# A macaron block on one core: expert blocks taken in packs of up to four instead of one at a time

## What is computed

```python
x = x + 0.5 * ffn(layernorm(x)); x = x + attn(layernorm(x)); x = x + 0.5 * ffn(layernorm(x))
def ffn(x):                      # both times the same weights; 8 experts, H = 512
    probs = softmax(xf @ router_w.T); topv, topi = top_k(probs, 2)
    topv = topv / (topv.sum(-1, keepdims=True) + 1e-9)
    h = gelu(einsum('td,edh->teh', xf, w1), exact)     # only the two chosen experts count
    return sum over the two chosen e of topv_e * (h_e @ w2[e])
```

## Time and profile before

| | us |
|---|---|
| median of 3 runs | 418.84 |
| the runs | 416.03, 418.84, 419.93 |
| the profiled execution | 416.92 |
| its span, first to last instruction | 415.2 |
| first expert phase, about | 25 to 185 |
| attention, both groups, about | 185 to 264 |
| second expert phase, about | 264 to 402 |

### The profile page before, as it was taken

One profiled execution on the slowest core, in us unless ns is written; L12 is line 12 of the kernel. 1 busy time (PEld: TensorE's weight loads), 2 busy tenths in 40 slices (PEclk: granted clock), 3 DMA queues, 4 the chain that ended last, 5 costly groups with the idle time before them and its releaser, 6 DMA issues.

```text
span 415.2 us, 6711 instructions
## 1 busy us (share of the span) xinstructions
PE 278.6 (67%) x1985; PEld 253.5 (61%) x1986; DVE 152.0 (37%) x675; ACT 143.9 (35%) x280; POOL 159.5 (38%) x187
## 2 busy tenths in 40 slices
PE   3226359981399359997376781599718998878650
PEld 2216359971299259985165551499618998878640
DVE  5691015710111013574169651557002221312234
ACT  4212125521154035653133241275114564434220
POOL 4447710067414720007702477001760006566650
PEclk9999559996589658999575787789856999889785
DMA  7913231122195210111100011112211222222115
GB/s 252 321 34 95 52 33 34 34 59 57 44 211 183 58 44 27 38 41 46 52 6 0 2 44 51 47 33 58 83 51 55 76 66 70 59 70 77 57 38 171
DMA packets 34254, 29.33 MB, mean 71 GB/s; under 512 B 4824, under 2 KB 29152, under 8 KB 34224
## 3 DMA queue, kind: packets, MB, share of 16 engines
q1 hardware_dynamic: 29312, 18.65, 15.0%
q0 software_dynamic: 4768, 9.78, 9.8%
q10 hardware_dynamic: 144, 0.52, 0.3%
HBM read 15.68 MB, written 13.26 MB: 70 GB/s over the span
## 4 chain that ended last, share of the span: by engine, by line
PE 51%; another core or an unknown queue 18%; issue 13%; DVE 10%; DMA 3%; ACT 2%; ACTq 1%; POOL 1%; SPq 0%; DVEq 0%; POOLq 0%
PE bank L1073 20%; PE bank L1085 18%; PE bank L1064 3%; PE bank L1143 2%; DVE xs L871 2%; PE bank L1030 2%; PE bank L1123 2%; PE bank L1014 2%; PE bank L1107 1%; PE bank L1133 1%; ACT w_block L567 1%; DVE xa L732 1%; DMA router_rows<-in_L_ffn_router_w 1%; DMA y_rows<-final_rows 1%
## 5 line engine op out<-in xcount | busy, mean ns | idle before, releaser
L1073 PE MATMUL bank<-xT,w_block 128*128 128x128 f32 x736 | 113.8, 300 | 37.8 <-issue 27.0
L1073 PEld LDWEIGHTS bank<-xT,w_block 128*128 128x128 f32 x736 | 102.8, 214 | 41.4 <-issue 36.5
L1085 PE MATMUL bank<-w_sb,act 128*128 x736 | 109.2, 296 | 19.5 <-issue 11.2
L1085 PEld LDWEIGHTS bank<-w_sb,act 128*128 128x128 f32 x736 | 100.0, 211 | 23.9 <-issue 23.9
L573 ACT ACTIVATE act<-bank 128x512 f32<-128x512 f32 x92 | 54.9, 597 | 157.8 <-PE bank L1073 72.1
L857 DVE COPY yb<-bank 128x128 f32<-128x128 f32 x92 | 26.6, 290 | 183.9 <-PE bank L1085 91.6
L500 POOL DMA_INDIRECT y_rows<-slots_out,slot_of x48 | 45.9, 957 | 64.9 <-DMA slots_out<-yb 50.9
L476 POOL DMA_INDIRECT xb_first<-xn_rows,row_in x46 | 43.6, 949 | 57.7 <-issue 42.9
L567 ACT COPY w_block<-w_sb 128x512 f32 x92 | 56.4, 613 | 20.7 <-issue 20.4
L511 POOL DMA_INDIRECT final_rows<-yb,row_of x23 | 22.4, 974 | 52.0 <-DVE row_of L847 38.2
L844 DVE COPY xT<-bank 128x128 f32<-128x128 f32 x92 | 26.1, 283 | 20.4 <-remote 13.4
(11 more groups left out here) (124 smaller groups left out, 243.5 us busy)
## 6 DMA issues: line engine op xcount, KB each, us to landing
slots_out<-yb SPq DMA_DIRECT2D x69, 64.0 KB
w_sb<-in_L_ffn_w SPq DMA_DIRECT2D x8, 512.0 KB, 7.4
xb_numbered<-numbered_slots SPq DMA_DIRECT2D x23, 64.5 KB
slots_in<-w_sb SPq DMA_DIRECT2D x4, 368.0 KB
xb_numbered<-slots_in SPq DMA_DIRECT2D x23, 64.0 KB
numbered_slots<-numbered SPq DMA_DIRECT2D x3, 387.0 KB
xs<-in_L_attn_x SPq DMA_DIRECT2D x4, 256.0 KB, 3.4
out<-xs SPq DMA_DIRECT2D x8, 128.0 KB
```

The lines of the kernel that those rows point to most:

```text
L1073: mm = nc.tensor.matmul(h_ps[k][:, q * P:(q + 1) * P], w1_block[c2 % UNROLL][:, q * P:(q + 1) * P], xT[c2 % UNROLL][:], start=True, stop=True)
L1085: mm = nc.tensor.matmul(y_ps[k][:, 0:D], act[c3 % UNROLL][:, q * P:(q + 1) * P], w2_sb[:, bass.ds(at + q * D, D)], start=(q == 0), stop=(q ...
```

## The change

The 46 blocks of a phase are cut into 14 packs of 1, 2, 4, 4, 4, 4, 4 and 4, 4, 4, 4, 4, 2, 1 blocks; seven packs are a group. A pack has one PSUM bank for its turned rows (there is one such bank, where there were two of one block each) and one for its results (there are two), and each is copied by one VectorE instruction. First products have four banks. `w1_block` and `act` exist eight times, `xT_pack` twice, `xb_pack` and `yb_pack` three times. TensorE makes the first products of pack n with the second products of pack n-1 between them, and turns pack n+1 behind the second first product of pack n. SyncE's loads and stores take a pack each, 256 KB for four blocks. The waits of `gather_in` are once a pack: for the pack four before to have landed, and in group 1 for the turn of the last pack whose buffers it overwrites. In the tail, four gathers come first and then, behind the final stores of each pack, three. All steps are written out; there are no loops. Positions of work beside the steps shift a little, two PSUM banks of the second normalisation and the turned attention weights move, and the products of blocks 2 and 3 of a phase wait for that normalisation's copies. The core of the diff, cut, in the order constants, banks, SyncE, GpSimd (two places), ScalarE, VectorE, TensorE; `turn_at` is 1, and 0 in a pack of one block:

```diff
-LAG = 4
-UNROLL = 4
+PACK = 4
+PACK_SIZES = [1, 2] + [PACK] * 10 + [2, 1]
+H_BANKS = 4
+WIDE_BUFS = 8
+PACK_BUFS = 3
+FETCH_SEMS = 4
...
+        RETURNED_FIRST, RETURNED_BESIDE = 4, 3
...
-        xT_ps, h_ps, y_ps = bank[0:2], bank[2:4], bank[4:6]
+        xT_ps, y_ps = bank[0], (bank[1], bank[4])
+        h_ps = (bank[2], bank[3], bank[5], bank[6])
...
+            def load(n):
+                k, size = n % PACK_BUFS, len(blocks_of(n))
+                if n >= LAST_PACKS + PACK_BUFS:
+                    sp.wait_ge(row_known, n - LAST_PACKS - PACK_BUFS + 1)
+                elif n >= PACKS + PACK_BUFS:
+                    sp.wait_ge(xT_ready, n - PACK_BUFS + 1)
...
+            for n in range(PACKS, LAST_PACKS + 1):
+                if n + 2 < LAST_PACKS:
+                    load(n + 2)
+                if n + 1 == LAST_PACKS:
+                    sp.wait_ge(scattered[1], 16 * TOP * GT)
+                    load(n + 1)
+                    load(n + 2)
+                if n == LAST_PACKS:
+                    load(n + 2)
+                if n > PACKS:
+                    store(n - 1)
+            for n in range(LAST_PACKS + 3, 2 * PACKS):
+                load(n)
...
-                for b in range(MAX_BLOCKS):
-                    c = g * MAX_BLOCKS + b
-                    if c >= UNROLL:
-                        pool.wait_ge(x_fetched[c % UNROLL], 16 * (c // UNROLL))
-                    if g:
-                        pool.wait_ge(xT_ready, b + 1)
+                if g:
+                    pool.wait_ge(xT_ready, pack_of(blocks_of(n)[-1] - MAX_BLOCKS) + 1)
+                if n >= FETCH_SEMS:
+                    pool.wait_ge(x_fetched[n % FETCH_SEMS], 16 * transfers_until(n - FETCH_SEMS, 0, FETCH_SEMS))
+                for c in blocks_of(n):
...
-            for b in range(MAX_BLOCKS):
-                store_final(b)
-                if b % FINAL_PACE:
-                    next(returning, None)
+            some_of(returning, RETURNED_FIRST)
+            for n in range(LAST_PACKS, 2 * PACKS):
+                store_final(n)
+                some_of(returning, RETURNED_BESIDE)
...
+                for c in range(first, end):
+                    gelu(c)
+                    if c + H_BANKS < end:
+                        copy_w1(c + H_BANKS)
+                    beside(c - first + 2)
...
+                for n, turn_at in first_product_at(m):
+                    for j, c in enumerate(blocks_of(n)):
+                        beside(c - first + 2)
+                        if j == turn_at and n + 1 < (m + 1) * PACKS:
+                            copy_xT(n + 1)
+                    if n > m * PACKS:
+                        copy_y(n - 1)
...
+                for n, turn_at in first_product_at(m):
+                    behind = len(blocks_of(n - 1)) if n > m * PACKS else 0
+                    for j in range(max(len(blocks_of(n)), behind)):
+                        if j < len(blocks_of(n)):
+                            first_product(n, j)
+                        if j == turn_at and n < last_pack:
+                            turn(n + 1)
+                        if j < behind:
+                            second_product(n - 1, j)
+                        if j < len(blocks_of(n)):
+                            beside(PACK_STARTS[n] + j - first + 2)
```

More of the change, by code:

```diff
@@ L39 @@
 MAX_BLOCKS = (GT * P * TOP + (P - 1) * E) // P
[L40 to L47 removed]
+OFFSETS = 4
+BLOCKS = GROUPS * MAX_BLOCKS
+PACK = 4
+PACK_SIZES = [1, 2] + [PACK] * 10 + [2, 1]
+assert sum(PACK_SIZES[:7]) == MAX_BLOCKS and sum(PACK_SIZES) == BLOCKS
+PACKS = len(PACK_SIZES)
+GROUP_PACKS = PACKS // GROUPS
+PACK_STARTS = [m * BLOCKS + sum(PACK_SIZES[:n]) for m in range(2) for n in range(PACKS)]
+LAST_PACKS = 2 * PACKS - GROUP_PACKS
+H_BANKS = 4
+WIDE_BUFS = 8
+PACK_BUFS = 3
+FETCH_SEMS = 4
 FILL_PARTS = 4
@@ new lines, in transfers_until, with packs_until, first_product_at, offset_reader @@
+        def transfers_until(n, first, sems):
+            return sum(len(blocks_of(p)) for p in range(first, n + 1) if p % sems == n % sems)
+        def packs_until(n, first):
+            return len([p for p in range(first, n + 1) if p % PACK_BUFS == n % PACK_BUFS])
+        def first_product_at(m):
+            for n in range(m * PACKS, (m + 1) * PACKS):
+                yield n, min(1, len(blocks_of(n)) - 1)
+        def offset_reader(eng, regs, m):
+            known = {}
+            def at(c):
+                b = c - m * BLOCKS
+                if b % MAX_BLOCKS % OFFSETS == 0:
+                    if b == MAX_BLOCKS:
+                        eng.wait_ge(routed, GROUPS * (m + 1))
+                    n = min(OFFSETS, MAX_BLOCKS - b % MAX_BLOCKS)
+                    eng.load(regs[:n], expert_at[0:1, b:b + n])
+                    for j in range(n):
+                        known[c + j] = eng.snap(regs[j], min_val=0, max_val=(E - 1) * H)
+                return known[c]
+            return at
@@ L396, in _ @@
-            first_expert_phase()
-            last_expert_phase()
+            for n in range(PACKS):
+                store(n)
+                if FIRST_FILL <= n < FIRST_FILL + FILL_PARTS:
+                    fill_part(2 * (n - FIRST_FILL))
+                    fill_part(2 * (n - FIRST_FILL) + 1)
+            sp.wait_ge(scattered[0], 16 * TOP * GT)
+            load(PACKS)
+            load(PACKS + 1)
+            for n in range(PACKS, LAST_PACKS + 1):
[9 more added lines that the diff above has]
+                    store(n - 1)
@@ L494, in gather @@
                 g = p % GROUPS
-                for k in range(UNROLL):
-                    done = len([G for G in range((p + 1) * MAX_BLOCKS) if G % UNROLL == k])
-                    pool.wait_ge(y_stored[k], 16 * done)
+                end = (p + 1) * GROUP_PACKS
+                for n in range(end - PACK_BUFS, end):
+                    pool.wait_ge(y_stored[n % PACK_BUFS], 16 * packs_until(n, 0))
                 for t in range(GT):
```

380 lines of the change are left out of this document (168 added, 212 removed).

## The result

The changed kernel took 430.43 us (median of 4 runs, 429.22 to 432.64) against 418.60 for the kernel before beside it (416.03 to 419.93): ratio 1.0296, 95% interval 1.0227 to 1.0365. It is slower by 12 us; the forecast was 416.8, no change, in a range of 404 to 426. Two further measurements of the changed kernel on other chips gave ratios of 1.0298 (c0) and 1.0359 (e0).

What follows compares the result with a forecast made beforehand. It took TensorE to be bound at 1.90 us a block, plus losses beside GpSimd's unbroken indirect transfers. Terms 0 - 2.0 + 0 + 2.5 - 2.5 = -2.0 on 416.92 gave 414.9, or 416.8 as median; range 404 to 426.

Steps and rivals of the forecast that it cites:

- Undisturbed blocks at 1.90: Expert phases away from GpSimd's transfers: a block takes 1.90 us, TensorE is full, and the change leaves this untouched.
- Copies and turns in fours: VectorE copies and TensorE turns per four blocks: hidden behind TensorE, worth 0, range -1 to +2 us.
- Four banks: First products: more banks and buffers give 0 in long runs of transfers, and 0.9 us in each short one.
- short trains: Seven back-to-back indirect transfers in the tail: some 0.55 us lost per transfer, 3.9 in all, 3.0 after the change.
- Train 1: First gather of x, 23 back-to-back transfers: nothing ahead of it changes, so 0, range -2 to +2 us.
- Train 2 ... breaks: Second gather of x, 23 transfers: splits into 16 and seven, 20.8 us lost against 22.8, so -2.0, range -4 to +3.
- SyncE's order: Last group's first pack: its load stands behind a store, so TensorE waits; +2.5 us, range 0 to +4.
- Trains 3 to 6: Later runs of back-to-back transfers before the tail, two of 16: same counts and nearly the same starts, so 0.
- The tail: From group 0's last y copy to the last final store: packs of seven transfers, -2.5 us, bounds +16 and -12.
- The slower rival: Tail: GpSimd need not pause, so runs of 14 transfers cost 1.1 us each, 9.4 more, 426 us; chance 0.24.
- Depth cures the short trains: Beside transfers: four banks let TensorE run on, about 402 us (chance 0.14), or 409 at half effect (0.20).
- Trains are not the cause: Whole kernel: losses come from depth alone, so most of 37.8 us idle before first products goes; under 395, chance 0.03.

Runs made afterwards that it cites:

- c0: The changed kernel, not edited, measured again on another chip as a control: 429.32 us, ratio 1.0298 to the kernel before.
- e0: The changed kernel, not edited, measured again on one chip beside e1 and e2: 436.25 us, ratio 1.0359 to the kernel before.
- e1: The changed kernel with the norm of group 0's attention begun a block earlier, two pieces a step: 434.98 us, ratio 1.0231 to the kernel before.
- b1: The kernel before with the norm of group 0's attention begun at step 48 instead of 45: 421.80 us, ratio 1.0135.
- e2: The changed kernel with early norm, copy of turned rows before the routing piece, and last group's first load a pack earlier: 426.10 us, ratio 1.0117.
- a2: The changed kernel with VectorE's copy of turned rows placed ahead of the routing piece: 432.57 us, ratio 1.0296 to the kernel before.
- c1: The changed kernel with two banks for first products instead of four: 431.27 us, ratio 1.0318 to the kernel before.
- a3: The changed kernel with SyncE's load of the last group's first pack issued one pack earlier: 434.58 us, ratio 1.0372 to the kernel before.
- b2: The kernel before with GpSimd's 16 gathers of group 0's results in phase 1 paused for later y copies after every four: 407.32 us, ratio 0.9769.
- d1: The kernel before with the second gather of x, phase 1's return of group 0's results and phase 2's first 16 transfers sent in fours: 377.96 us, ratio 0.9058.
- d2: As d1, on the kernel before, with the first gather of x also sent as eight, then fours: 364.80 us, ratio 0.8798.
- the repairs: The three edits of e2 on the changed kernel: early norm, copy of turned rows first, last group's first load a pack earlier; 426.10 us.

## Why the prediction was wrong

By its steps. One reading first: TensorE's digit is not between 0 and 3 in all the slices in which GpSimd's is 6 or 7. At the head of a long train it is still 6 to 9, and it falls to 1 or 3 in the next slice; in the tail, where GpSimd pauses often, it stays at 6 to 8. That row already pointed at the unbroken length.

- **Undisturbed blocks at 1.90**: right. The changed kernel goes through blocks 31 to 38 at 15.0 us for eight where no train runs, a little under 1.90 each.
- **"Copies and turns in fours ... I take 0, range -1 to +2"**: this step failed, and it is the one that took the time out of the range: it stands at 0 for stretches that cost 5.2 and 2.3 of the 12.3, and without these the sum would be +4.8. It costed the instructions and not their place in VectorE's order. Two things sat in that place. The diff moves the last combine from step 44 to 45 and the norm from 45 to 46, while the steps now run to 47 instead of 49; I gave that no term at all. Undone, it is worth up to 1.3% (e1 against e0), and done alone to the kernel before, three steps later, which leaves it as few steps to the end of the phase, it costs 1.35% (b1). And the copy of turned rows stands behind the routing piece; the step named the two starts as the only place where cover could be gone and then dismissed it, "since turns for the router stand between". Those very turns and logits were what the copy waited behind. With the copy first beside the other two, block 46 to block 60 takes 2.9 less (e2 against e0), with the copy first alone 2.2 less (a2 against the result's run).
- **"Four banks": 0 in long trains**: right by c1, which has two and costs nothing measurable. That short trains get 0.9 cheaper has no support: 62.7 (c0), 64.4 (the result's run) and 64.9 (e0) for the tail with four banks, 64.8 with two. The limit of about 33 unseen matmuls was not tested.
- **"Train 1", 0, range -2 to +2**: the y copy of block 10 came 4.4 later, of which 1.8 are the order of the products; the other 2.6 are above the range, but most of them are back by the end of the phase.
- **"Train 2 ... breaks", -2.0**: wrong. 23 transfers went in one piece, from 81.87 to 110.26. Its stretch costs 1.3 more than before, less than the 2.5 that the prediction had for an unbroken one (it took 1.1 a transfer for that, where its own 22.8 for 23 transfers are 1.0):

```profile
81.87 0.94 POOL L463 DMA_INDIRECT xb_first<-xn_rows,row_in  x1 [27.87 <-DVE row_in L816]
...
109.32 0.94 POOL L463 DMA_INDIRECT xb_first<-xn_rows,row_in  x1 [0.30 <-issue]
```

- **"SyncE's order", +2.5**: right. The wait is 1.77 and the stretch 2.2 longer; with the load a pack earlier the stretch is back to 15.2 (a3). The 1.1 for two issues named no row; in the run the store and the load's two issues take from 334.84 to 336.38.
- **"Trains 3 to 6 ... 0"**: the count of transfers was right, and train 3's stretch got 1.6 cheaper (with two banks in c1 as well, so it isn't depth), but what stands beside them was not looked at. Train 4 began 2.3 behind the last y copy in either kernel; what changed was how far attention had come by then.
- **"The tail", -2.5**: wrong size. From the start of block 68's y copy to the end of the last final store: 65.0 before, 65.1 after, where the prediction's terms without the 1.8 for the order of products, which stand in the stretch up to block 60, are 58.2 + 2.5 = 60.7. TensorE's last y copy starts 54.8 behind that of block 68, against 62.0 before, and GpSimd takes it all. Its restarts, and its last transfer:

```profile
356.85 1.00 POOL L487 DMA_INDIRECT y_rows<-slots_out,slot_of  x1 [39.45 <-DMA slots_out<-yb_pack]
...
376.08 0.99 POOL L498 DMA_INDIRECT final_rows<-yb_pack,row_of  x1 [5.57 <-DVE yb_pack L861]
...
387.70 0.99 POOL L498 DMA_INDIRECT final_rows<-yb_pack,row_of  x1 [3.03 <-DVE yb_pack L861]
...
399.14 0.99 POOL L498 DMA_INDIRECT final_rows<-yb_pack,row_of  x1 [2.72 <-DVE row_of L850]
...
415.66 0.96 POOL L498 DMA_INDIRECT final_rows<-yb_pack,row_of  x1 [0.30 <-issue]
```

  39 transfers at 1.25 are 48.8, the three waits 11.3, and the first gather starts 4.6 behind block 68: 64.7. The first 11 and the last 14 go without a pause. That is one execution: in c0, the same kernel, GpSimd sent 4, 7, 7, 7, 11, 2 and 1, TensorE's last y copy started 61.4 behind block 68's and the last final store waited for it, and the tail was no longer (63.4 by the same count). So no run shows that the one or the other engine always ends the tail. The row behind its cost of short trains was not a train of seven by itself either: GpSimd sent five, paused for 0.55 and sent two. And its 2.05 for a product is a length in the timeline, where an undisturbed one is 1.06, not 0.89. The slower rival ("GpSimd's packs set the tail") describes the result's run, in which its sign, more than seven transfers without a pause, was there; but its price of 9.4 didn't arise, and it is not why the kernel is slower.
- **The other rivals.** "Depth cures the short trains" (0.34 of the chance) has c1 against it, as its 3 for each of trains 3 and 6 is not there. "Trains are not the cause" has b2, d1 and d2 against it: nothing but the pauses was changed there.
- **The sum.** With the terms as measured: end of phase 1 +1.1, attention +5.2, block 46 to 60 +4.1, SyncE's order +2.2, tail -0.3, all together +12.3 on the profiled 416.92: 429.2, where 429.44 was measured.

On their chip the repairs take back 10.2 of 14.6 (e2 against e0). About 1% stays: attention in e2 still takes 89.6 against the 85.6 of the kernel before. I haven't found why; the traces differ in how attention's waits fall against trains 4 and 5, and the same code there took from 90.6 to 95.8 in the profiled runs of the changed kernel and its variants with the late norm, and from 88.5 to 89.9 in those with the early one. That is argued from traces and was not tested.

The prediction was right about what owns the lost third of TensorE's time (long unbroken trains, 1.0 to 1.1 us a transfer), and wrong to treat that as a fixed cost. It assumed that pieces of seven cost 0.55 a transfer and never asked what the kernel would be worth if all trains were sent so.

## What to carry to other kernels

Unpaced back-to-back indirect transfers beside matmuls are the first thing to break up: a wait on the consumer's own progress after every four took 12% off this kernel (d2, 364.8 us, faster than both kernels), with no other change. When work is regrouped, write down the new order of every helper engine around each phase's first and last steps, and give each shifted constant a term of its own: in the kernel before the same instructions, three steps later, cost 1.35%. And ask of every saving what ends the tail; here, from the end of group 0, it took 62 to 67 us in all eighteen profiled runs, whatever came before and whichever engine was last.

## What the runs showed of the hardware that was not expected

How long GpSimd goes on without a pause matters more than how much it does. The same 16 transfers of train 3 cost 17.8 us in one piece and 9.1 as 8, 4 and 4 (b2); trains 2 and 3 together, 39 transfers, cost 39.4 and then 12.9 as pieces of 3 to 8 (d1). In an unbroken train TensorE sends single matmuls, as here in train 2 of the changed kernel:

```profile
98.14 0.37 PE L1105 MATMUL bank<-w_sb,act 128*128 x1 [1.03 <-issue]
99.54 0.37 PE L1105 MATMUL bank<-w_sb,act 128*128 x1 [1.03 <-issue]
```

They stand 1.4 or 0.7 us apart, with no wait that the trace can name. That they don't hang on how many banks are free was shown (c1, with two, has them too). What in the chip it is, was not. In the fours of d2 the interval between two transfers is what it was in long trains, 1.25 us, so GpSimd itself is not slowed by what runs beside it; the products are.

The Trainium skill's page "SBUF — State Buffer", section "SBUF: two separate sides", says that engine and DMA ports cannot contend, and explains one apparent slowdown, in which VectorE keeps GpSimd from writing a transfer's descriptors. The runs speak against reading that as "transfers cost the engines nothing", and the direction is the other way round here: it is the matmuls that wait (105.9 us for 35 blocks beside unbroken trains, 79.4 with the same transfers in pieces). That it is these ports at which they wait, no run shows.
